# Two expert layers with sorted dispatch: each dispatch scatter waits for the landing of the one before it

## The chip, the core and the metric

The kernel runs on one core of a Trainium2 chip. The metric is the device time of one execution in microseconds, given as the median over runs. The core's engines are TensorE (PE, with its weight loads as PEld), VectorE (DVE), ScalarE (ACT), GpSimd (POOL) and SyncE (SP); "q" behind an engine's name is its own DMA queue or its instruction sequencer. DMAs issued by SyncE and by GpSimd are carried out by 16 shared DMA engines.

## What is computed

4096 tokens of width 128 (32 tiles of 128 tokens, in 128 batches of 32) pass two layers with a residual each. Cut to what matters:

```python
# layer 0: weights by batch, then 16 experts, one per token, and a shared expert
h   = einsum('bnc,bcd->bnd', x, w[subject]) + b[subject]
e   = top_1(h @ w_router.T);  s = sigmoid(logit of e)
y   = down_e(up * silu(gate)) of the row s*h  +  shared(h)
x   = x + y
# layer 1: adapter and norm by batch, then 8 experts, two per token, capacity 1280 rows each
h   = layernorm(x + relu(x @ W1[lang] + b1) @ W2[lang] + b2) * gamma + beta
y   = g1 * expert_e1(h) + g2 * expert_e2(h) + 0.1 * shared(h)   # a row past the capacity is dropped
x   = x + y
```

## The kernel before

**Dispatch.** Each layer sorts its tokens by expert in HBM. For each tile of 128 tokens VectorE computes a slot per token (`slot`), ScalarE copies the token rows, with a code and the score behind them, to `disp` (130 floats a row), and GpSimd issues one indirect DMA, a scatter, that writes the tile's 128 rows of 520 bytes to their slots in `rows0` (layer 0) or `rows1` (layer 1).

- Layer 0: 32 scatters at line 571, in four rounds of eight (`RT` = 8). A round begins when VectorE has its slots (`slots0`, line 918) and ScalarE its rows and scores. The scatters increment the semaphores `sc0[0]` and `sc0[1]`, by turns of four tiles (`G` = 4).
- Layer 1: 64 scatters at line 605, 32 for the tokens' first choice (`k` = 0) and 32 for the second. The first choice has rounds of 8, 8, 8, 4 and 4 tiles, each waiting for its slots (`slots1`, line 1072); the second choice's slots come all at once (line 1177). The semaphores are `sc1[k][half]`. Twice, GpSimd rewrites the codes of one half of `disp` between scatters (line 612).

Between the two dispatches GpSimd's program has the 48 scatters back of layer 0's results (line 582) and six residual additions (line 376); after them come the 80 scatters back of layer 1 (line 623).

**Who waits for a dispatch.** SyncE's program is in order too. It waits until all scatters of layer 0 have landed (both `sc0` at their full count), then loads blocks of 128 sorted rows (line 450, `blk_x`). In layer 1 it waits for all four `sc1` in the same way, then loads groups of 256 sorted rows (line 487, `grp_x`).

**TensorE.** In layer 0 it transposes x (line 1304), applies the weights by batch (line 1361), computes the router logits (line 1380), then the shared expert of six of the eight groups of four tiles (lines 1393 and 1402). Then come the 48 blocks: a transpose of the block as its first step (line 1304 with `blk_x`), gate and up (lines 1426 to 1428), down (line 1441). In layer 1 it runs adapter, norm and logits for eight groups (lines 1545 to 1589), the shared expert (up in lines 1517 to 1519, down in line 1603), of which most lies in a loop, and then 40 groups of sorted rows: a transpose (line 1304 with `grp_x`), up (lines 1633 to 1635), down (line 1645). Its first transpose of a group stands ahead of the last shared product.

VectorE's output of a group is `grp_y` (line 1236). At the end the results are read back, weighted and stored. SyncE also issues, early in layer 0, the zero fills of `rows0`, `rows1` and `back1` (lines 413, 426, 429) and the loads of all expert weights of layer 0 (lines 420 and 423).

Of the kernel before, what the change touches and what calls it, by code (L numbers as in the profile page):

```python
# [5 lines left out]
def adaln_moe_two_layers(  # L6
# [44 lines left out]
    S = T // B  # L51
    NSUB = c0_w.shape[0]
    E0, _, F0x2 = f0_gate_up.shape
    F0 = F0x2 // 2
    C0 = F0 // P
    NLANG = c1_b2.shape[0]
    A = c1_w1.shape[1] // NLANG
    E1, _, F1 = f1_w1.shape
    C1 = F1 // P
    TOP_K = 2  # L60
# [7 lines left out]
    NT = T // P  # L68
    G = 4
# [41 lines left out]
    with ctx:  # L111
# [3 lines left out]
        def sem(name):  # L115
            return ctx.enter_context(nc.semaphore(name))
# [174 lines left out]
        sc0 = [sem(f"sc0_{k}") for k in range(2)]  # L291
# [47 lines left out]
        sc1 = [[sem(f"sc1_{k}{h}") for h in range(2)] for k in range(2)]  # L339
# [190 lines left out]
        def _(pool):  # L530
# [35 lines left out]
            for t in range(NT):  # L566
                if t % RT == 0:
                    pool.wait_ge(slots0, t // RT + 1)
                    pool.wait_ge(scored, t // RT + 1)
                    pool.wait_ge(tok_done, (t + RT) // G)  # L570
                gp.indirect_dma_start(rows0, bass.IndirectOffsetOnAxis(ap=slot[:, 0, t:t + 1], axis=0),  # L571
                                      disp[:, t, :], None, bounds_check=NBLKP * P - 1,
                                      oob_is_err=False).then_inc(sc0[t // G % 2], 16)
# [22 lines left out]
            HT = NT // 2  # L596
            for k in range(TOP_K):
                for t in range(NT):
                    if k == 0 and t in first_tiles:
                        r = first_tiles.index(t)  # L600
                        pool.wait_ge(slots1, r + 1)
                        pool.wait_ge(b_tk, (t + round_tiles[r]) // G)
                    if k == 1 and t == 0:
                        pool.wait_ge(slots1, NR1 + 1)
                    gp.indirect_dma_start(rows1, bass.IndirectOffsetOnAxis(ap=slot[:, k, t:t + 1], axis=0),  # L605
                                          disp[:, t, :], None, bounds_check=E1 * CAP - 1,
                                          oob_is_err=False).then_inc(sc1[k][t // HT], 16)
                    if (k, t) in ((0, NT - 8), (1, HT - 8)):
                        h = k
                        pool.wait_ge(sc1[0][h], 16 * HT)  # L610
                        half = slice(h * HT, (h + 1) * HT)
                        gp.tensor_scalar(disp[:, half, H:H + 1], codes[:, half].unsqueeze(2), float(-T), None,
                                         ALU.add).then_inc(codes1, 1)
                        pool.wait_ge(codes1, h + 1)
# [687 lines left out]
        def _(pe):  # L1302
# [33 lines left out]
            for n in range(NG + 1):  # L1336
# [11 lines left out]
                if n < NG:  # L1348
                    pe.wait_ge(xT_done, n + 1)
                    if n == 0:  # L1350
                        pe.wait_ge(ld_c0w, 16)
                        pe.wait_ge(off_ready, 1)
                    _, offs = nc.values_load_multi_w_load_instructions(
                        w0off[0:1, n * GB:(n + 1) * GB], engines=(mybir.EngineType.PE,), min_val=0,
                        max_val=(NSUB - 1) * H, skip_runtime_bounds_check_because="subjects are under NSUB")
                    for b in range(QB):
                        if b == 1 and n >= 3 and n % 2 == 1:
                            rank0((n - 3) // 2)
                        for i in range(G):
                            t = i * QB + b  # L1360
                            last = mm(PS[1 + b][0:S, i * H:(i + 1) * H],  # L1361
                                      xT[n % 2][:, t * S:(t + 1) * S], c0w[:, ds(offs[t], H)],
                                      start=True, stop=True)
                        last.then_inc(pe_c, 1)
# [363 lines left out]
```

## Time and profile before

| | |
|---|---|
| Median of 3 runs | 573.94 us (572.52 to 575.43) |
| Span of the profiled execution | 571.1 us |
| TensorE, matmuls | 463.1 us, 81% of the span, 3132 instructions |
| VectorE | 261.9 us, 46% |
| ScalarE | 255.9 us, 45% |
| GpSimd | 238.0 us, 42%, 255 instructions |
| Granted TensorE clock, mean | 0.909 |
| DMA | 62.33 MB, 109 GB/s on the mean |

The profiled execution's own device time isn't given beside its span; the median of the runs lies 2.8 us above the span. Times in a trace count from the span's start. A row of the timeline has the start, the busy time, engine, line, operation, what it writes and reads, and in brackets how long the engine sat idle before and what ended that. "issue" is a time in which the engine waited for nothing that the profile shows. A transfer's own time isn't in its issuing row; the DMA views and the chain of waits show it. On 40 slices of the span a digit is a busy share in tenths.

### The profile page before, as it was taken

How to read it: one execution, taken by the hardware profiler on the slowest of the kernel's cores; microseconds unless marked ns; L12 is line 12 of the kernel's file. 1: busy time of each engine (PE TensorE's matmuls, PEld its weight loads, DVE VectorE, ACT ScalarE, POOL GpSimd, SP SyncE). 2: the span in 40 equal slices, each digit the busy share in tenths (PEclk: the TensorE clock that was granted, in tenths of full speed). 3: DMA queues.
4: the chain of work that ended last, by engine and by line, in shares of the span. 5: the costliest groups of instructions: out<-in, count | busy, mean ns of one | idle time of the engine just before them, and what ended most of it. 6: DMA issues, size and time to landing. Idle time of an engine off the chain costs nothing.

```text
span 571.1 us, 10130 instructions
## 1 busy us (share of the span) xinstructions
PE 463.1 (81%) x3132; PEld 392.7 (69%) x3133; DVE 261.9 (46%) x831; ACT 255.9 (45%) x596; POOL 238.0 (42%) x255
## 2 busy tenths in 40 slices
PE   6897698978888889999846765489999999999910
PEld 3785564566676766787744655178999999999900
DVE  1144267845555554347447912053433333233475
ACT  2453453235555543556314241034455555555653
POOL 2023535214554555003272777600155555556550
PEclk8997879999999999999787796579999999999975
DMA  9999921102222107400010111110223434313569
GB/s 242 365 340 368 367 66 37 39 23 67 74 71 63 47 11 235 143 2 20 19 51 15 48 48 55 42 47 1 61 76 96 134 107 113 105 50 88 165 182 282
DMA packets 70930, 62.33 MB, mean 109 GB/s; under 512 B 9676, under 2 KB 57439, under 8 KB 70898
## 3 DMA queue, kind: packets, MB, share of 16 engines
q1 hardware_dynamic: 63202, 48.32, 28.5%
q0 software_dynamic: 7168, 12.56, 6.7%
q10 hardware_dynamic: 528, 1.05, 0.6%
q8 instruction: 17, 0.28, 0.2%
q14 instruction: 15, 0.12, 0.1%
HBM read 32.44 MB, written 31.69 MB: 112 GB/s over the span
## 4 chain that ended last, share of the span: by engine, by line
PE 63%; another core or an unknown queue 10%; DVE 9%; DMA 7%; issue 6%; ACT 2%; POOL 1%; SPq 0%; DVEq 0%; POOLq 0%; ACTq 0%
PE PS L1645 11%; PE PS L1304 8%; PE PS L1361 6%; PE PS L1603 5%; PE PS L1441 3%; PE PS L1635 3%; PE PS L1565 3%; PE PS L1633 3%; PE PS L1634 3%; PE PS L1393 2%; PE PS L1402 2%; DMA back1b<-grp_y,grp_i 2%; PE PS L1426 2%; PE PS L1428 1%
## 5 line engine op out<-in xcount | busy, mean ns | idle before, releaser
L623 POOL DMA_INDIRECT back<-grp_y,grp_i x70 | 69.8, 997 | 93.9 <-DVE grp_y L1236 71.0
L605 POOL DMA_INDIRECT rows<-disp,slot x64 | 63.6, 994 | 76.1 <-DVE slot L1072 56.0
L1645 PE MATMUL PS<-w2r,act 128*128 128x128 f32 x640 | 78.1, 275 | 0.5 <-ACT act L789 0.5
L1645 PEld LDWEIGHTS PS<-w2r,act 128*128 128x128 f32 x640 | 74.8, 192 | 0.9 <-DVE grp_y L1236 0.7
L582 POOL DMA_INDIRECT back<-act,blk_i x48 | 46.9, 977 | 60.8 <-DVE act L1015 41.1
L789 ACT ACTIVATE act<-PS,b1r 128x256 f32<-128x256 f32 x160 | 63.7, 477 | 16.5 <-PE PS L1635 14.2
L571 POOL DMA_INDIRECT rows<-disp,slot x32 | 32.6, 1018 | 67.4 <-issue 53.8
L1236 DVE TENSOR_TENSOR grp_y<-PS,b2r 128x256 f32<-128x256 f32 x40 | 17.0, 424 | 89.6 <-PE PS L1645 69.5
L1603 PE MATMUL PS<-sw,act 128*128 128x128 f32 x256 | 37.5, 313 | 14.1 <-issue 11.8
L1633 PE MATMUL PS<-xh,w1h 128*128 128x256 f32 x160 | 48.3, 302 | 0.0
L740 ACT ACTIVATE act<-PS,sb 128x512 f32<-128x512 f32 x32 | 21.4, 688 | 59.6 <-remote 32.9
L1603 PEld LDWEIGHTS PS<-sw,act 128*128 128x128 f32 x256 | 36.5, 228 | 15.4 <-issue 13.5
L1635 PE MATMUL PS<-xh,w1l 128*128 128x256 f32 x160 | 45.2, 283 | 0.0
L643 ACT ACTIVATE xh<-PS 128x256 fp32r<-128x256 f32 (+1 forms) x48 | 20.1, 419 | 55.9 <-PE PS L1304 48.2
L1634 PE MATMUL PS<-xl,w1h 128*128 128x256 f32 x160 | 44.9, 281 | 0.0
L1361 PE MATMUL PS<-c0w,xT 128*32 x256 | 38.7, 321 | 7.4 <-issue 7.4
L1361 PEld LDWEIGHTS PS<-c0w,xT 128*32 128x32 f32 x256 | 32.5, 131 | 12.4 <-issue 9.3
L1441 PEld LDWEIGHTS PS<-w_dn,act 128*128 128x128 f32 x192 | 25.8, 190 | 15.5 <-issue 14.7
L1441 PE MATMUL PS<-w_dn,act 128*128 x192 | 30.9, 283 | 5.5 <-ACT act L643 5.2
L1008 DVE SCALAR_TENSOR_TENSOR act<-PS,blk_x,act 128x256 f32<-128x256 f32 x48 | 23.2, 483 | 20.2 <-ACT act L697 15.7
L643 ACT ACTIVATE t<-PS 32x512 f32<-32x512 f32 x32 | 18.7, 584 | 29.0 <-PE PS L1361 20.7
L1148 DVE SCALAR_TENSOR_TENSOR acc<-PS,acc 128x512 f32<-128x512 f32 x8 | 5.5, 690 | 54.9 <-remote 38.5
(256 smaller groups left out, 1009.9 us busy)
## 6 DMA issues: line engine op xcount, KB each, us to landing
rows<-zrow SPq DMA_DIRECT2D x32, 260.0 KB, 5.0
grp_x<-rows SPq DMA_DIRECT2D x40, 130.0 KB
w_raw<-in_f_gate_up SPq DMA_DIRECT2D x8, 512.0 KB, 10.1
back<-zrow SPq DMA_DIRECT2D x8, 512.0 KB
back<-back SPq DMA_DIRECT2D x16, 256.0 KB, 5.0
blk_x<-rows SPq DMA_DIRECT2D x48, 65.0 KB
acc<-in_x SPq DMA_DIRECT2D x8, 256.0 KB, 5.8
y0g<-back SPq DMA_DIRECT2D x8, 256.0 KB, 3.2
```

The source lines that it names most:

```text
L582: gp.indirect_dma_start(back0, bass.IndirectOffsetOnAxis(ap=blk_i[c][:, 0:1], axis=0), blk_y[s][:, :], None, bounds_check=last_token, oob_ ...
L605: gp.indirect_dma_start(rows1, bass.IndirectOffsetOnAxis(ap=slot[:, k, t:t + 1], axis=0), disp[:, t, :], None, bounds_check=E1 * CAP - 1, ...
L623: gp.indirect_dma_start(back, bass.IndirectOffsetOnAxis(ap=grp_i[v % NX][:, u:u + 1], axis=0), grp_y[k][:, u, :], None, bounds_check=last, ...
L789: sc.activation(act[k][:, c, 0:UP], PS[1 + k * (C1 // 2) + c // 2][:, (c % 2) * UP:(c % 2 + 1) * UP], ACT.Silu, bias=b1r[e][:, c:c + 1]).t ...
L1304: return nc.tensor.transpose(dst, src, ident[0:k, 0:k])
L1361: last = mm(PS[1 + b][0:S, i * H:(i + 1) * H], xT[n % 2][:, t * S:(t + 1) * S], c0w[:, ds(offs[t], H)], start=True, stop=True)
L1441: last = mm(PS[4 if k == 0 else 7][:, 0:H], blk_aT[k][:, c * P:(c + 1) * P], w_dn[:, ds(off + c * H, H)], start=c == 0, stop=c == C0 - 1)
L1603: last = mm(tile(PS[4], i), tile(act[k][:, c, :], i), sw2[:, c, :], start=c == 0, stop=c == C1 - 1)
L1633: mm(y, high, xh[k][:, 0:UP], start=True, stop=False)
L1634: mm(y, high, xl[k][:, 0:UP], start=False, stop=False)
L1635: last = mm(y, low, xh[k][:, 0:UP], start=False, stop=True)
L1645: last = mm(PS[5 + k][:, u * P:(u + 1) * P], act[k][:, c, u * P:(u + 1) * P], w2r[e][:, c, :], start=c == 0, stop=c == C1 - 1)
```

## The change

Ahead of each scatter but the first of a layer, GpSimd waits until the semaphore of the scatter before it has reached that scatter's count: 31 waits in layer 0, 63 in layer 1. The scatters, their order, their semaphores and all other engines' programs stay. In layer 1 the first scatter of the second choice waits for the last one of the first.

```diff
@@ layer 0 dispatch, GpSimd
                     pool.wait_ge(tok_done, (t + RT) // G)
+                if t >= 1:
+                    pool.wait_ge(sc0[(t - 1) // G % 2], 16 * ((t - 1) // (2 * G) * G + (t - 1) % G + 1))
                 gp.indirect_dma_start(rows0, bass.IndirectOffsetOnAxis(ap=slot[:, 0, t:t + 1], axis=0),
                                       disp[:, t, :], None, bounds_check=NBLKP * P - 1,
                                       oob_is_err=False).then_inc(sc0[t // G % 2], 16)
@@ layer 1 dispatch, GpSimd
                     if k == 1 and t == 0:
                         pool.wait_ge(slots1, NR1 + 1)
+                    if (k, t) > (0, 0):
+                        kl, tl = divmod(k * NT + t - 1, NT)
+                        pool.wait_ge(sc1[kl][tl // HT], 16 * (tl % HT + 1))
                     gp.indirect_dma_start(rows1, bass.IndirectOffsetOnAxis(ap=slot[:, k, t:t + 1], axis=0),
                                           disp[:, t, :], None, bounds_check=E1 * CAP - 1,
                                           oob_is_err=False).then_inc(sc1[k][t // HT], 16)
```

## Rows read from the trace of the kernel before

**Rows 1.** The page: its head, and the DMA business in 40 slices of 14.3 us

```profile
span 571.1 us, 10130 instructions
...
DMA  9999921102222107400010111110223434313569
```

**Rows 2.** The page, costliest groups: busy us, mean ns, idle before

```profile
L605 POOL DMA_INDIRECT rows<-disp,slot x64 | 63.6, 994 | 76.1 <-DVE slot L1072 56.0
```

**Rows 3.** Timeline of GpSimd, layer 0's dispatch: start us, busy us

```profile
38.86 1.18 POOL L571 DMA_INDIRECT rows<-disp,slot  x1 [33.99 <-issue]
...
79.30 0.98 POOL L571 DMA_INDIRECT rows<-disp,slot  x1 [11.31 <-issue]
80.58 0.98 POOL L571 DMA_INDIRECT rows<-disp,slot  x1 [0.30 <-issue]
...
93.86 0.98 POOL L571 DMA_INDIRECT rows<-disp,slot  x1 [4.59 <-DVE slot L918]
...
103.39 1.50 POOL L571 DMA_INDIRECT rows<-disp,slot  x1 [0.30 <-issue]
```

**Rows 4.** Timeline of GpSimd, layer 1's dispatch

```profile
265.26 0.99 POOL L605 DMA_INDIRECT rows<-disp,slot  x1 [36.61 <-DVE slot L1072]
...
284.99 0.97 POOL L605 DMA_INDIRECT rows<-disp,slot  x1 [9.79 <-DVE slot L1072]
...
309.64 1.37 POOL L605 DMA_INDIRECT rows<-disp,slot  x1 [9.64 <-DVE slot L1072]
...
368.15 0.98 POOL L605 DMA_INDIRECT rows<-disp,slot  x1 [0.30 <-issue]
```

**Rows 5.** Timeline of SyncE's queue: first block loads, first group loads

```profile
106.35 17.63 SPq L450 DMA_DIRECT2D blk_x<-rows  x6
...
370.50 31.80 SPq L487 DMA_DIRECT2D grp_x<-rows  x6
```

**Rows 6.** Timeline of TensorE: first block, two shared products, first group

```profile
119.56 0.33 PE L1304 MATMUL PS<-ident,blk_x 128*128 128x128 f32 x1 [0.78 <-DVE acc L964]
...
374.50 5.45 PE L1603 MATMUL PS<-sw,act 128*128 128x128 f32 x32 [0.82 <-DVE acc L1150]
...
382.60 3.73 PE L1603 MATMUL PS<-sw,act 128*128 128x128 f32 x32
...
398.92 0.38 PE L1304 MATMUL PS<-ident,grp_x 128*128 128x128 f32 x2
```

**Rows 7.** DMA queues, packets: 38.86 to 41.00; 38.86 to 43.00; 79.30 to 81.25

```profile
q1 hardware_dynamic: 300, 0.61, 104.1%
...
q0 software_dynamic: 37, 0.08, 6.7%
...
q0 software_dynamic: 32, 0.07, 10.4%
```

**Rows 8.** The chain of waits: start us, us of three transfers

```profile
122.83 1.82 DMA blk_x<-rows
...
211.68 2.08 DMA back<-act,blk_i
...
213.85 2.88 DMA y0g<-back
```

**Rows 9.** Timeline of VectorE: two steps that give slots to waiting GpSimd

```profile
92.89 0.17 DVE L918 CAST slot<-slotF 128x8 int32<-128x8 f32 x1
...
264.22 0.17 DVE L1072 TENSOR_SCALAR slot<-slotF 128x8 int32<-128x8 f32 x1
```

**Rows 10.** Three windows: length, busy us of PE, PEld, DVE, ACT, POOL; PEclk, DMA share, GB/s

```profile
336.90:344.60 7.70, 0.15 (x1) 0.00 (x0) 1.45 (x3) 0.07 (x1) 5.61 (x7) 0.73 0.13 43
350.00:372.60 22.60, 8.46 (x19) 4.70 (x19) 0.00 (x0) 1.38 (x2) 14.75 (x15) 0.58 0.17 54
374.50:398.90 24.40, 24.40 (x164) 22.77 (x165) 10.27 (x21) 9.12 (x14) 0.00 (x0) 0.93 0.00 1
```

## The prediction

> **What bounds the kernel now.** I began with the page: a span of 571.1 us, and the strip of DMA business, where the slices up to 71 us (five of 14.3 us each) stand at nine tenths and the rest far lower [rows 1]. The costliest groups show the edited instructions: the 64 scatters of L605, 63.6 us of work, 994 ns each [rows 2]. GpSimd is busy 42% of the span, so a share says little; what counts is whether the two dispatches end in time for whoever waits for all of them.
>
> I then followed GpSimd in order of time. In layer 0 it issues four rounds of eight scatters. The first scatter starts at 38.86. Within a round one follows the other at 1.28 us (0.98 of work, 0.30 of idle time), as from 79.30 to 80.58; between rounds it waits for slots; the last starts at 103.39 [rows 3]. In layer 1 the 64 scatters start at 265.26, the rounds whose slots come late at 284.99 and 309.64, and the last at 368.15 [rows 4]. SyncE waits for every landing of a layer and only then loads rows: it issues the first block load at 106.35 and the first group load at 370.50, which is 2.35 us after the start of the last scatter of layer 1 [rows 4, 5].
>
> Last I looked at the consumer. TensorE takes the first block at 119.56 and the first group at 398.92 [rows 6]. Neither waits for the dispatch. With a small load taking 1.82 us [rows 8], the first block has been there since about 108.3, so layer 0 has 11 us of slack. For layer 1 I take 2.4 us for the 130 KB group load, between 1.82 us for 65 KB and 2.88 us for 256 KB [rows 8]; it has been there since 372.9, so the slack is 26.0 us. The bound is now the chain of TensorE and the engines that feed it. The dispatch lies beside it, with these two slacks.
>
> **The change, part by part.** It removes nothing and moves nothing. It adds 31 waits in layer 0 and 63 in layer 1, all on GpSimd's queue, each for the landing of the scatter just issued. Semaphore and count name just that scatter, so no wait is satisfied early. Behind each wait stands the next scatter, so a chain of issue, landing and wake replaces a chain of issues. The cost of the 94 wait instructions themselves is taken as nothing: GpSimd would be waiting for the landing at that time anyway.
>
> *Landing, nothing else on the DMA queues.* The chain shows the last scatter back of layer 0 starting at 211.68 and landing 2.08 us later [rows 8]. It moves 512 bytes per row where the edited ones move 520. For the edited ones, all 32 packets of the scatter of 79.30 are done in the window that ends at 81.25, 1.95 us after its start [rows 7]; that is the lower bound, 1.9. SyncE's 2.35 holds its own reaction too [rows 4, 5]; that is the upper bound. I take 2.1.
>
> *Wake.* No row shows GpSimd woken by its own DMA. The nearest shows it woken by VectorE: the slots of L918 end at 93.06 and the scatter starts at 93.86, 0.80 us later [rows 3, 9]; L1072 ends at 264.39 and the scatter starts at 265.26, 0.87 us later [rows 4, 9]. The 0.30 between two scatters without a wait [rows 3] is the floor: there the next instruction is already at the engine, and with a wait it can't be. I take 0.8.
>
> So one cycle is **2.9 us** instead of 1.28, with bounds of 1.9 + 0.8 = 2.7 and 2.35 + 0.87 = 3.2.
>
> *Landing under load.* Until about 71 us other transfers fill the DMA engines [rows 1]. Of the first scatter, started at 38.86, no packet is seen by 41.00 and the 32nd only shortly before 43.00 (37 by then, some of them the second scatter's) [rows 7]. That is 4.1 us to land, and a cycle of 4.9. Five packets too many by then may mean a landing somewhat earlier, and the wait for the semaphore somewhat later: bounds 3.4 and 5.0 for the landing, 4.2 and 5.8 for the cycle. Seven cycles fall into this stretch: 38.86 + 7 × 4.9 = 73.2.
>
> The DMA page of the Trainium skill (DMA: Bandwidth & Descriptors, section Queues, rings and completion order) says that each DMA engine takes turns between its queues, packet by packet. By that rule a scatter with two packets on each engine would wait for two foreign ones, 0.12 us each (300 packets in 2.14 us on 16 engines) [rows 7], land after about 2.3 us and not 4.1, and the sum would be 12.6 us smaller, an estimate of 645 us. The trace disagrees with so small a delay.
>
> *Layer 0.* All later rounds have their slots (79.30, 93.86) before GpSimd gets to them. The last scatter starts at 38.86 + 7 × 4.9 + 24 × 2.9 = 142.8. Add 2.35 until SyncE issues and 1.9 for the load: TensorE takes the first block at 147.0 instead of 119.56, **+27.4 us**. The 11 us of slack are used up in this number.
>
> *Layer 1.* Every slot is ready before its turn again: round two would begin at 288.5 (ready at 284.99), the 25th scatter at 334.9 (ready at 309.64). Counted from the same start, the last one starts at 265.26 + 63 × 2.9 = 448.0. With 2.35 and 2.4 the first group is taken at 452.7 instead of 398.92, **+53.8 us**. The two copies of L612 between scatters ran while nothing waited for them; now they run during a landing, at no cost.
>
> *Clock.* TensorE now idles some 27 us before the blocks and much longer before the groups. After the idle stretch up to 374.50 one shared product took 5.45 us, and the next 3.73 us [rows 6]: 1.7 us for running below the full clock. Twice that is 3.4; the block stage is not bound by TensorE alone, so I take **3 us** in all.
>
> *The sum.* 27.4 + 53.8 + 3.0 = 84.2 us on a span of 571.1, so 655.3. The median of the runs, 573.94, is 2.8 above the span. That gives **658 us** for the changed kernel.
>
> *A gain that the longer cycle may bring.* While layer 1's scatters come every 1.28 us, TensorE is all but still from 336.9 to 344.6 and does little from 350 to 372.6; when they have ended it is busy all the time [rows 10]. If spaced scatters free it, it reaches the first group some 30 us earlier and waits there for the dispatch. I cost it at nothing, since the dispatch is then what comes last by 53.8 us or more.
>
> **The rivals.**
> A. *Short cycle.* GpSimd is woken by a landing almost as fast as it passes from one scatter to the next (0.30). The cycle is 2.4, under load 4.4. Layer 0: 38.86 + 30.8 + 57.6 + 4.25 = 131.5, +12.0. Layer 1: 265.26 + 151.2 + 4.75 = 421.2, +22.3. With the clock 37, so 611 us. For it: the 0.30 is a real row. Against it: both wakes on record are 0.80 or more.
> B. *The stillness of TensorE lasts as long as the scatters do*, or the cycle lies above 3.2. In the first case TensorE is only freed 4.5 us after the last scatter's start, as now (368.15 to 372.6), and still has the 26.3 us from there to 398.92 before it: 448.0 + 30.8 = 478.8, 26 us more than in the sum, 684 us. Against it: in the pauses between the rounds TensorE ran well, and the new cycle is pause for two thirds.
> C. *Load costs a scatter nearly nothing*: its few packets slip in between the others, the loaded cycle is 3.1 us and not 4.9, and 7 × 1.8 = 12.6 us go from the sum: 645 us. For it: a scatter has only two packets on each engine (32 in all) [rows 7]. Against it: the first scatter's late packets.
> D. *Faster.* The cycle is so short that the dispatch stays hidden, and TensorE's stillness goes. The point of decision: the last scatter of layer 1 must start by 398.92 − 4.75 = 394.2, so a cycle under (394.2 − 265.26) / 63 = 2.05 us. At 1.6 us, with the 25th scatter at 309.64, the last would start at 372.0 and the first group be taken at 376.8, 22 us earlier: 552 us. Against it: a landing alone was 2.08 us.
> E. *The waits pass early* and nothing changes: 574 us. Only a miscounted semaphore could do that.
>
> **How the numbers follow.** Forecast 0.60, A 0.13, B 0.16, C 0.07, D 0.03, E 0.01. At both lower bounds (2.7; 4.2) the sum is 38.86 + 29.4 + 64.8 + 4.25 = 137.3, +17.8, and 265.26 + 170.1 + 4.75 = 440.1, +41.2, with the clock 62: 636 us. At both upper bounds (3.2; 5.8) it is 160.5, +41.0, and 471.6, +72.7, with the clock 117: 691 us. The range takes these in and about half of A: 622 to 692 us. About 0.5% is what a measurement of this kernel can tell from no change. Faster by more than that is D, 0.03; within it E, 0.01; slower everything else, 0.96.
>
> **What the new profile would show.** Scatters of a round 2.7 to 3.2 us apart in both layers, wider apart before 71 us. SyncE's first block load near 145, and its first group load near 370.5 + 79.8 + 27.4 + 1.5 = 479. TensorE idle before the first block and before the first group, released there by the load. If scatters stand 2.4 us apart, A is right. If TensorE still does shared products after the first group has landed, B. If the first eight scatters are spaced like the rest, C. The prediction is wrong at its root if the first group is taken without a wait for the load.

## Result and profile after

| | before | after |
|---|---|---|
| Median, 4 runs each | 573.5 us | 687.65 us (685.92 to 689.23) |
| Ratio, 95% interval | | 1.2015 [1.1955, 1.2075] |
| Profiled execution, own time and span | -, 571.1 us | 686.79, 684.7 us |
| First block taken | 119.56 | 161.04 |
| First scatter of layer 1 | 265.26 | 307.74 |
| First group taken | 398.92 | 514.77 |
| From there to the end of the span | 172.2 | 169.9 |

The kernel is slower by 114 us. The forecast was 658, the range 622 to 692. Each ratio here and below is taken from executions in the chip's faster state alone and can differ by some tenths of a per cent from the quotient of the medians. The four differences between the lines of the table are +41.5, +1.0, +73.4 and -2.3; they sum to the 113.6 us between the spans.

The page, now in slices of 17.1 us, shows two holes in TensorE's strip: at 0 from 120 to 154 us and from 411 to 513. The DMA strip, nine tenths at the start as in [rows 1], is near nothing in both.

```profile
span 684.7 us, 10136 instructions
...
PE   6888893005888889999779910000009999999940
...
DMA  9999200001222207100000000000003343333198
```

The timeline of GpSimd after the change (start us, busy us, engine, line, operation, idle before and releaser), layer 0 and then layer 1, to be read against [rows 3, 4]:

```profile
41.46 1.18 POOL L573 DMA_INDIRECT rows<-disp,slot  x1 [36.53 <-issue]
48.25 0.98 POOL L573 DMA_INDIRECT rows<-disp,slot  x1 [5.61 <-DMA rows<-disp,slot]
...
72.70 0.97 POOL L573 DMA_INDIRECT rows<-disp,slot  x1 [2.77 <-DMA rows<-disp,slot]
75.76 0.97 POOL L573 DMA_INDIRECT rows<-disp,slot  x1 [2.09 <-DMA rows<-disp,slot]
...
91.87 0.97 POOL L573 DMA_INDIRECT rows<-disp,slot  x1 [2.32 <-DMA rows<-disp,slot]
96.95 0.98 POOL L573 DMA_INDIRECT rows<-disp,slot  x1 [4.10 <-DMA rows<-disp,slot]
...
156.77 0.97 POOL L573 DMA_INDIRECT rows<-disp,slot  x1 [2.18 <-DMA rows<-disp,slot]
...
307.74 0.99 POOL L610 DMA_INDIRECT rows<-disp,slot  x1 [36.61 <-DVE slot L1077]
310.84 0.98 POOL L610 DMA_INDIRECT rows<-disp,slot  x1 [2.11 <-DMA rows<-disp,slot]
...
510.08 0.98 POOL L610 DMA_INDIRECT rows<-disp,slot  x1 [2.07 <-DMA rows<-disp,slot]
```

Each scatter is now released by the landing of the one before. The first five cycles average (72.70 − 41.46) / 5 = 6.25 us (four of 6.6 to 7.2 and a fifth of 3.82), the next 26 average 3.23, and the 63 of layer 1 average (510.08 − 307.74) / 63 = 3.21 us.

The chain of waits splits one quiet cycle (start us, us, what):

```profile
141.24 2.29 DMA rows<-disp,slot
143.53 0.02 issue
143.55 0.03 POOLq L573
143.58 0.73 issue
144.31 2.29 DMA rows<-disp,slot
```

2.29 us from the scatter's start to its landing, 0.78 us until GpSimd starts the next: 3.07 us.

SyncE's queue and TensorE, against [rows 5, 6]:

```profile
159.19 19.28 SPq L450 DMA_DIRECT2D blk_x<-rows  x13
...
512.42 3.57 SPq L487 DMA_DIRECT2D grp_x<-rows  x6
```

```profile
161.04 0.45 PE L1309 MATMUL PS<-ident,blk_x 128*128 128x128 f32 x1 [50.87 <-DMA blk_x<-rows]
...
386.75 3.73 PE L1608 MATMUL PS<-sw,act 128*128 128x128 f32 x32
393.13 3.73 PE L1608 MATMUL PS<-sw,act 128*128 128x128 f32 x32
...
514.77 0.66 PE L1309 MATMUL PS<-ident,grp_x 128*128 128x128 f32 x2 [117.91 <-DMA grp_x<-rows]
```

TensorE waits 50.9 us for the first block and 117.9 us for the first group. That is more than the kernel lost. The shared products (line 1608) now follow each other every 6.38 us: the still stretches of [rows 10], in which TensorE was held up, are gone, and the time won there goes into the longer wait.

### The profile page after: what moved, and what is told of

Its sections match the earlier page's. It is cut to its first block, busy times and chain, and to the rows that moved or that the text cites. A ratio compares the mean times of both kernels' runs of the same rounds, so it can differ in the third digit from the quotient of the medians.

```text
span 684.7 us, 10136 instructions
## 1 busy us (share of the span) xinstructions
PE 450.3 (66%) x3132; PEld 385.8 (56%) x3133; DVE 260.0 (38%) x831; ACT 256.1 (37%) x596; POOL 235.7 (34%) x255
## 4 chain that ended last, share of the span: by engine, by line
DMA 40%; PE 38%; issue 14%; DVE 2%; ACT 2%; another core or an unknown queue 2%; POOLq 1%; SPq 0%; POOL 0%; DVEq 0%; ACTq 0%
DMA rows<-disp,slot 36%; PE PS L1650 8%; PE PS L1309 6%; PE PS L1446 3%; PE PS L1640 2%; PE PS L1639 2%; PE PS L1638 2%; PE PS L1366 2%; PE PS L1570 2%; PE PS L1431 2%; PE PS L1433 1%; DMA back1b<-grp_y,grp_i 1%; PE PS L1432 1%; DMA acc<-in_x 1%
## 5 line engine op out<-in xcount | busy, mean ns | idle before, releaser
L1309 PE MATMUL PS<-ident,grp_x 128*128 128x128 f32 x80 | 15.6, 278 | 119.2 <-DMA grp_x<-rows 117.9
L1309 PEld LDWEIGHTS PS<-ident,grp_x 128*128 128x128 f32 x80 | 10.0, 143 | 119.7 <-issue 119.2
L1309 PE MATMUL PS<-ident,blk_x 128*128 128x128 f32 x48 | 14.1, 293 | 56.3 <-DMA blk_x<-rows 51.1
L1216 DVE TENSOR_SCALAR grp_i<-grp_x 128x2 int32<-128x2 f32 x35 | 6.1, 174 | 115.3 <-DMA grp_x<-rows 115.3
L1309 PEld LDWEIGHTS PS<-ident,blk_x 128*128 128x128 f32 x48 | 7.0, 146 | 58.4 <-issue 57.5
L1366 PE MATMUL PS<-c0w,xT 128*32 x256 | 33.7, 294 | 8.1 <-issue 8.1
L1008 DVE TENSOR_TENSOR blk_xl<-PS,blk_xh 128x128 fp32r<-128x128 f32 x48 | 14.0, 291 | 65.6 <-ACT blk_xh L648 58.2
L648 ACT ACTIVATE blk_xh<-PS 128x128 fp32r<-128x128 f32 x48 | 13.2, 274 | 62.3 <-PE PS L1309 61.2
L1366 PEld LDWEIGHTS PS<-c0w,xT 128*32 128x32 f32 x256 | 29.5, 119 | 11.5 <-issue 10.0
```

Of the source, the lines that this page charges most:

```text
L648: return sc.activation(dst, src, ACT.Copy)
L1309: return nc.tensor.transpose(dst, src, ident[0:k, 0:k])
L1366: last = mm(PS[1 + b][0:S, i * H:(i + 1) * H], xT[n % 2][:, t * S:(t + 1) * S], c0w[:, ds(offs[t], H)], start=True, stop=True)
```

## Experiments

Ratios are to the kernel before as run beside each: medians 571.15 us for e1 to e4, 571.08 for e5 to e8, 574.25 for e9 to e11.

### Each layer's waits alone

e1 is the changed kernel without its wait in layer 1:

```diff
-                    if (k, t) > (0, 0):
-                        kl, tl = divmod(k * NT + t - 1, NT)
-                        pool.wait_ge(sc1[kl][tl // HT], 16 * (tl % HT + 1))
```

e2 is the changed kernel without its wait in layer 0:

```diff
-                if t >= 1:
-                    pool.wait_ge(sc0[(t - 1) // G % 2], 16 * ((t - 1) // (2 * G) * G + (t - 1) % G + 1))
```

> The 31 waits of layer 0 alone, layer 1 as before. Theory (a chain of issue, landing and wake that shows only past the slack): the first block is taken 41 to 42 us later than before, as in the changed kernel (161.0 against 119.6), and nothing else grows, since layer 1's scatters run at 1.28 us again: about 615 us. TensorE's still stretches in layer 1 are back. Rival (the two layers' costs are not additive: layer 0's delay is partly taken back by a shift of layer 1's work against its dispatch, or made larger by a cold clock): under 608 or over 622 us.

> The 63 waits of layer 1 alone, layer 0 as before. Theory: the dispatch takes 63 cycles of 3.2 us instead of 103 us in all, less the slack of 26 us: the first group is taken 73 us later than before relative to the dispatch's start, the work after it takes 2 us less, so about 645 us, and with e1 the two sum to the 114 us of the changed kernel. TensorE's shared products run through without a still stretch and then wait over 100 us for the first group. Rival (the still stretches come from what TensorE and ScalarE do and not from the scatters' spacing): TensorE still stands still for some 30 us, which costs no time here but is seen in the trace.

e1 took 612.33 us (ratio 1.0720 [1.0663, 1.0776]) and e2 644.89 us (1.1312 [1.1230, 1.1394]). That is 41.2 and 73.7 us over 571.15, together 114.9, against 114.15 for both. Both times are as expected, and the costs add: each is one dispatch past its own slack. In e1 the first block is taken at 161.07, and with scatters 1.28 us apart TensorE is held up again in layer 1: it sits idle for 13.56 us ahead of the shared product at 417.82. In e2 it is not held up, and then waits:

```profile
352.45 3.73 PE L1606 MATMUL PS<-sw,act 128*128 128x128 f32 x32
469.68 0.66 PE L1307 MATMUL PS<-ident,grp_x 128*128 128x128 f32 x2 [113.50 <-DMA grp_x<-rows]
```

### What makes the first landings late

The changed kernel, with the zero fills of lines 426 and 429 moved behind the first weight loads of layer 1.

```diff
-            for r in range(0, E1 * CAP, P * 4):
-                sp.dma_start(rows1[r:r + P * 4, :].rearrange("(p a) r -> p (a r)", p=P),
-                             zrow[:, 0:zw]).then_inc(zero1, 16)
-            for r in range(0, TOP_K * T, P * 8):
-                sp.dma_start(back1[r:r + P * 8, :].rearrange("(p a) h -> p (a h)", p=P),
-                             zrow[:, 0:8 * H]).then_inc(zero1, 16)
...
+            for r in range(0, E1 * CAP, P * 4):
+                sp.dma_start(rows1[r:r + P * 4, :].rearrange("(p a) r -> p (a r)", p=P),
+                             zrow[:, 0:zw]).then_inc(zero1, 16)
+            for r in range(0, TOP_K * T, P * 8):
+                sp.dma_start(back1[r:r + P * 8, :].rearrange("(p a) h -> p (a h)", p=P),
+                             zrow[:, 0:8 * H]).then_inc(zero1, 16)
             for k in range(TOP_K):
                 for h in range(2):
                     sp.wait_ge(sc1[k][h], 16 * (NT // 2))
```

> The changed kernel with the zero fills of rows1 and back1 (9.4 MB) issued behind layer 1's first weight loads instead of early in layer 0. Theory (the first scatters land late because the DMA engines are full of these fills): no cycle of layer 0 is 6 us any more, all are 3.1 to 3.4, the last scatter starts at about 141 instead of 156.8, and the kernel takes about 672 us. Rival (a landing of the first round is late for another reason, for instance the first use of the queue or ScalarE's and VectorE's work at that time): the first five cycles stay above 5 us and the time is 686 to 690 us. The fills at their new place may hold the start of layer 1's dispatch by a few us.

675.22 us, ratio 1.1823 [1.1758, 1.1889]: 11 to 12 us less than the change, by the ratios and by the medians (687.65, ratio 1.2015; measured at another time). GpSimd's timeline, layer 0:

```profile
39.46 1.18 POOL L573 DMA_INDIRECT rows<-disp,slot  x1 [34.58 <-issue]
45.47 0.98 POOL L573 DMA_INDIRECT rows<-disp,slot  x1 [4.83 <-DMA rows<-disp,slot]
49.70 0.98 POOL L573 DMA_INDIRECT rows<-disp,slot  x1 [3.25 <-DMA rows<-disp,slot]
53.25 0.97 POOL L573 DMA_INDIRECT rows<-disp,slot  x1 [2.57 <-DMA rows<-disp,slot]
```

The third cycle is 3.55, and the last scatter starts at 144.08. So the fills made most of the early landings late. The theory had wanted the first two cycles short too, and the first is still 6.0 us. Weight loads remain there: SyncE's queue fills 53% of the DMA engines' time in that cycle. That the first use of the queue is slow in itself, the rival's example, does not fit a later run: in e11, which also has the late fills, the first scatter starts 2.6 us later (42.07), and the third, which waits for it, starts at 45.56; less the 0.78 us of its wake, the first had landed within 2.7 us.

### A wait that reaches further back

Here each scatter waits for the one two before it. Two scatters are then in flight, so they need semaphores of their own: four by turns in each layer. These waits also cover the one ahead of line 612.

```diff
-        sc0 = [sem(f"sc0_{k}") for k in range(2)]
+        sc0 = [sem(f"sc0_{k}") for k in range(4)]
...
-            for k in range(2):
-                sp.wait_ge(sc0[k], 16 * (NT // 2))
+            for k in range(4):
+                sp.wait_ge(sc0[k], 16 * (NT // 4))
...
+                if t >= 2:
+                    pool.wait_ge(sc0[(t - 2) % 4], 16 * ((t - 2) // 4 + 1))
...
-                                      oob_is_err=False).then_inc(sc0[t // G % 2], 16)
+                                      oob_is_err=False).then_inc(sc0[t % 4], 16)
...
+                    f = k * NT + t - 2
+                    if f >= 0:
+                        pool.wait_ge(sc1[f // 2 % 2][f % 2], 16 * (f // 4 + 1))
...
-                                          oob_is_err=False).then_inc(sc1[k][t // HT], 16)
+                                          oob_is_err=False).then_inc(sc1[t // 2 % 2][t % 2], 16)
...
-                        pool.wait_ge(sc1[0][h], 16 * HT)
```

> In both layers each scatter waits for the landing of the one two before it, with four semaphores by turns. Theory: two landings overlap, so the cycle falls to half, 1.55 to 1.65 us outside the loaded stretch. Layer 0: round four starts with its slots at 94 and ends at 106 to 107, hidden as before. Layer 1: from the slots at 309 on 39 cycles of 1.6, the last scatter at about 372 against 368 before, first group landed at 377. If the wider spacing takes TensorE's still stretches away, it reaches the first group before that and the kernel gains up to 22 us: about 552 us. Rival (the spacing of 1.3 and 1.6 us is the same to TensorE; only pauses of 2 us free it): 573 to 577 us.

545.94 us, ratio 0.9567 [0.9502, 0.9632]: **faster than the kernel before.** Layer 1's scatters run from 257.55 to 366.12; those of the second choice stand 1.63 us apart on average, from 1.28 to 2.3; in layer 0 the first block is taken at 112.19. TensorE:

```profile
343.16 3.73 PE L1607 MATMUL PS<-sw,act 128*128 128x128 f32 x32
370.76 0.66 PE L1308 MATMUL PS<-ident,grp_x 128*128 128x128 f32 x2 [23.86 <-DMA grp_x<-rows]
```

It runs through at 6.38 us a shared product, is done at 346.9, and waits for the group. Measured from layer 1's first scatter the first group comes after 113.2 us, against 133.7 before. The dispatch has become a little longer (108.6 us from first scatter to last, 102.9 before), and the kernel shorter, because before the bound was what the dispatch did to the other engines. The rival is out. The theory's 552 us was 6 too many: it gave layer 0 no gain, and it kept the slots of layer 1 as late as before. The first block came 7.4 us earlier, and the 21st scatter of layer 1, which waits for slots, started 36.8 us after the first, against 44.4 before.

> As e3, but each scatter waits for the one three before it. A landing and wake take 3.07 us, three spacings of 1.28 take 3.84, so the wait is met nearly always and the spacing stays 1.28 us, except behind a late landing. If the spacing is what makes TensorE stand still, the still stretches are back and the time is 568 to 575 us. If it is a pile of scatters behind a late landing that does it, the limit of three is enough, the dispatch ends near 362, and the kernel takes 540 to 546 us.

The same with 3 for 2: 559.18 us, 0.9784 [0.9691, 0.9876], faster than before, though not surely by 2%. In the quiet part of layer 1 the spacing is 1.28 us, and the still stretches are back:

```profile
329.28 5.35 PE L1607 MATMUL PS<-sw,act 128*128 128x128 f32 x32 [3.74 <-issue]
...
361.20 6.41 PE L1607 MATMUL PS<-sw,act 128*128 128x128 f32 x32 [19.01 <-DVE acc L1154]
```

The first group comes 129.8 us after the first scatter of layer 1 (256.75, 386.58). The first block is at 111.96: layer 0, where landings under load spaced the scatters at some 2 us, kept its gain of 7.6 us, most of the 12. So of the two expectations the first is right for layer 1. Its time, 568 to 575 us, was missed, chiefly because layer 0 gained.

> The wait for the one two before, in layer 1 alone; layer 0 unthrottled. Theory: layer 1's gain of e3 stays (first group 113 us after the dispatch's start, against 134 before), and layer 0's 7 us of e3 go (first block at 119.6 against 112.2): 551 to 555 us. Rival (layer 0 gave nothing in e3, its block start was only earlier by chance): 544 to 548 us.

The wait in layer 1 alone: 551.97 us, 0.9695 [0.9619, 0.9771], first block at 118.41. e3 was 6.0 us better, and its first block came 6.2 us earlier; that is layer 0's share, though the two were measured at different times and their intervals overlap a little. Why layer 0 gains was not tested. It looks like the same effect: from 60 to 80 us VectorE is busy for 7.80 us in the kernel before and for 14.17 us in e3.

### Is it the wait or the spacing

Both start from the kernel before and change layer 1 alone. `idle` is a new buffer that nobody reads. e6:

```diff
                                           oob_is_err=False).then_inc(sc1[k][t // HT], 16)
+                    for i in range(3):
+                        c = 3 * (NT * k + t) + i
+                        gp.memset(idle[:, c:c + 1], 0.0)
```

> No added wait at all: behind each scatter of layer 1 GpSimd writes three single columns of an unused buffer, which should space the scatters at 1.6 to 1.8 us. Theory (TensorE's still stretches come from scatters without a pause, and any pause takes them away): layer 0 as before, the last scatter of layer 1 at about 376, no still stretch, first group at about 381, 555 to 558 us. Rival (only the wait for a landing frees the engines): the still stretches last as long as the scatters, TensorE is freed at about 380 with 26 us of its work to do, 578 to 584 us.

568.87 us, 0.9983 [0.9945, 1.0021]. My spacing failed: the three writes slipped into the 0.30 us between two scatters, which stood 1.31 us apart and not the 1.6 to 1.8 expected.

```profile
350.99 0.98 POOL L606 DMA_INDIRECT rows<-disp,slot  x1 [0.16 <-issue]
351.94 0.20 POOL L611 MEMSET idle<- 128x1 f32 x3
352.30 0.98 POOL L606 DMA_INDIRECT rows<-disp,slot  x1 [0.16 <-issue]
```

The still stretches stayed (15.07 us before the product at 369.39), and the time, expected at 555 to 558 us, did not change. It tells nothing of wait against spacing.

e9:

```diff
                                           oob_is_err=False).then_inc(sc1[k][t // HT], 16)
+                    for i in range(1):
+                        c = 1 * (NT * k + t) + i
+                        gp.memset(idle[:, c:c + 1], 0.0).then_inc(idled, 1)
+                        pool.wait_ge(idled, c + 1)
```

> e6 spaced the scatters at 1.31 us only and left spacing and wait untold apart. Here GpSimd writes one column behind each scatter of layer 1 and waits for that write, never for a landing, which should space them at 2.0 to 2.1 us. Theory (spacing is what counts): no still stretch, TensorE is through with the shared expert near 350 and waits; with the slots of the late rounds at about 300 the last scatter starts at 380 to 390 and the first group is taken at 385 to 395: 558 to 568 us. Rival (only a wait for a landing frees the engines): the still stretches stay while scatters are issued, TensorE resumes behind them with some 26 us of work: 585 to 595 us.

568.29 us, 0.9944 [0.9893, 0.9996], at the upper edge of the 558 to 568 expected. Here GpSimd waits only for its own small write, and most scatters stand 1.89 us apart:

```profile
342.54 0.98 POOL L607 DMA_INDIRECT rows<-disp,slot  x1 [0.80 <-POOL idle L612]
343.51 0.12 POOL L612 MEMSET idle<- 128x1 f32 x1
344.43 0.98 POOL L607 DMA_INDIRECT rows<-disp,slot  x1 [0.80 <-POOL idle L612]
```

```profile
348.81 3.73 PE L1609 MATMUL PS<-sw,act 128*128 128x128 f32 x32
393.59 0.66 PE L1310 MATMUL PS<-ident,grp_x 128*128 128x128 f32 x2 [41.04 <-DMA grp_x<-rows]
```

No still stretch, with no wait for any landing. TensorE is done at 352.5 and waits 41 us for a dispatch that takes 125.8 us from first scatter to last, 23 us more than before. So no wait for a landing is needed; a pause between scatters is enough. It also shows that the gain is a balance: at 1.28 TensorE is held up, at 1.89 the dispatch is late by nearly as much, and at a mean of 1.63 (e3) the kernel is faster than at either.

### Versions that beat both kernels

> e3 with e4's late fills. In e3 TensorE waited 4.3 us for the first block, since the loaded stretch spaced layer 0's first scatters at up to 5 us. Theory: with the fills gone from there the first block is ready before TensorE, 4 us less, unless the fills at their new place hold back layer 1's dispatch: 539 to 543 us. Rival (the fills then collide with layer 1's start and the loads of its first experts, and the dispatch, which is the bound there, starts later): 546 to 555 us.

e3 with the late fills of e4: 538.32 us, 0.9435 [0.9359, 0.9510], 0.7 us below the range expected. The first block is taken at 106.81 without waiting for its load, and the late fills did not hold up layer 1.

> e8 without the wait on the last 12 scatters of layer 1. In e8 TensorE is through with the shared expert at about the time of the 52nd scatter and then waits 24 us for the first group, so nothing is left there that a denser spacing could hold up. Theory: 12 cycles of 1.29 instead of 1.62 us, 4 us less than e8: 533 to 536 us. Rival (the still stretch is then TensorE's last shared product or delays SyncE and the group loads): no gain, 537 to 541 us.

The edit against e8:

```diff
-                    if f >= 0:
+                    if 0 <= f < 50:
```

> e8's kernel once more, beside e10 on the same chip, to compare the two: 536 to 540 us, as in e8.

e10 took 534.13 us, 0.9273 [0.9224, 0.9322], and e8's kernel, run again beside it as e11, 538.73 us, 0.9363 [0.9327, 0.9398]. The last 12 scatters are 1.29 us apart, while TensorE has nothing left to do:

```profile
336.48 3.73 PE L1607 MATMUL PS<-sw,act 128*128 128x128 f32 x32
360.84 0.66 PE L1308 MATMUL PS<-ident,grp_x 128*128 128x128 f32 x2 [20.63 <-DMA grp_x<-rows]
```

The expected 4 us came (4.6), and the two intervals do not overlap. e10 is 7% below the kernel before, and its bound in layer 1 is the dispatch.

## Why the prediction was right, and where it was off

**The mechanism and the place were right.** Waits turn the dispatch into a chain of issue, landing and wake; the first block and the first group are released by their loads; nothing on the way is hidden beyond the slack. Both slacks were as read: e1 and e2 cost what the longer dispatch is past them.

**Cycle, 2.9 us: measured 3.21 in the mean of layer 1, 3.07 in a quiet cycle.** This is the step that was mis-sized, and most of the miss. The mean lies just above the stated upper bound of 3.2, and so over the line that the prediction drew for the second case of rival B.
- The wake, taken as 0.8 from GpSimd's waits for VectorE, was 0.78. Rival A, a wake of 0.30, is out.
- The landing, taken as 2.1, was 2.29. I had called the 2.35 us to SyncE's first load an upper bound that holds SyncE's reaction. The chain now shows that reaction as 0.08 us, so nearly all of the 2.35 was the landing. The 2.08 of a scatter back, whose rows are 512 bytes and not 520, had drawn me down. The Trainium skill's fit for such DMAs (DMA: Bandwidth & Descriptors, section Anatomy of one DMA — SWDGE (gpsimd) path), 2.0 us and the bytes at 436 GB/s, gives an estimate of 2.15 us for 66.6 KB; this trace is 0.14 above it.
- On top come late landings, 0.14 us a cycle. The longest of them stand beside packets of an instruction queue. The cycle from 91.87 to 96.95 is 5.08 us, and in the window 94.00 to 94.50 the instruction queue moves one packet of 0.02 MB; the cycle from 359.89 to 364.52 is 4.63 us, with a like packet between 361.00 and 361.50:

```profile
q8 instruction: 1, 0.02, 10.9%
...
q8 instruction: 1, 0.02, 14.4%
```

The Trainium skill (Runtime: NRT & Kernel Launch, section Instruction fetch mechanics) calls instruction fetches mostly hidden. Whether these two were not is open: no run tests that the packet is the cause, and the traces speak on both sides. In e2 three cycles of layer 1 hold such a packet (those from 264.48, 293.00 and 316.34) and take 3.13, 3.22 and 3.10 us; after the change the cycle from 336.15, with one, takes 4.44, and the one from 307.74, also with one, 3.10.

In the sum: layer 1's 63 cycles took 202.3 us and not 182.7, +19.6.

**Landing under load, 4.1 us, seven cycles: measured 5.8 to 6.4 us, four cycles, and one of 3.03.** The chain of waits after the change:

```profile
41.46 5.99 DMA rows<-disp,slot
...
48.25 5.80 DMA rows<-disp,slot
...
54.84 6.44 DMA rows<-disp,slot
...
62.06 6.03 DMA rows<-disp,slot
...
68.88 3.03 DMA rows<-disp,slot
...
72.70 2.28 DMA rows<-disp,slot
```

No q0 packet of the first scatter (41.46) is seen by 43.90, 28 by 45.90, 32 only by 46.90. Before, four scatters had started by 43.00, where I stopped counting, so the 37 packets seen by then need not hold all of the first one's. The five cycles, 6.25 us on average, lie above the stated upper bound of 5.8, but there were only five: 31.2 us in all, close to the 34.3 for seven of 4.9. That the two errors met is luck. e4 shows that the load is the cause. Rival C is out, and with it the estimate of a landing after 2.3 us under load, 645 us in all.

**Layer 0 in all, +27.4: measured +41.5.** From first to last scatter 115.3 us and not 103.9; 26 quiet cycles of 3.23 where 24 of 2.9 stood. Another 2.6 us is a later start of the first scatter (41.46 for 38.86); e1, with the same waits, had it at 40.75. From the last scatter to the first block 4.27, foreseen 4.25; layer 1's counterpart 4.69, foreseen 4.75.

**Clock, +3: nothing to see.** The first shared product after the wait takes 4.91 us at a granted clock of 0.75 where the one at 386.75 takes 3.73 at 1.00, but the stretches outside the dispatches grew by +1.0 and -2.3. The term is inside what two executions differ by.

**The gain costed at nothing** was real and worth nothing here, for the reason given. The first case of rival B is out: TensorE's shared products run through in e3, e9 and after the change, with scatters 1.63, 1.89 and 3.21 us apart. The text weighed the stillness as a risk; it was an opening. With a shorter wait the same effect makes the kernel faster than before, which rival D had tied to a cycle under 2.05 us. e3, with 1.63 us and 545.94 us, is that rival, reached by another wait. The bound of 2.05 was for a dispatch still hidden; in fact the limit is where the late dispatch costs more than the still stretches did. In e9, at 1.89 us, the two about balance.

**A miscount of the rounds.** Layer 1's first choice has rounds of 8, 8, 4, 4, 4 and 4 tiles, not 8, 8, 8, 4 and 4, so the scatter at 309.64 [rows 4] is the 21st and not the 25th. The forecast does not change: with cycles of 2.9 the 21st would start at 323.3, still later than its slots. Rival D does: at 1.6 us its last scatter comes at 309.64 + 43 × 1.6 = 378.4, the first group at 383.2, and the kernel takes 558 us and not 552.

With the measured cycles in the prediction's own formula, 41.46 + 31.2 + 26 × 3.23 + 4.25 = 160.9 (+41.3), and 265.26 + 63 × 3.21 + 4.75 = 472.2 (+73.3), the sum is 573.9 + 114.6 = 688.5 us. These terms are read from the run that they are to explain, so this shows that the formula is complete, not that it predicts.

## What to carry to other kernels

When each DMA waits for the one before, price a cycle as start to landing plus wake, both from the stretch in which it will run, and multiply by the length of the chain; then take off the slack of whoever waits for the last. The release of an engine that waits for a landing measures it: the chain shows how little of that interval is its own reaction. And look at what a dense run of small DMAs does to the other engines before treating its length as the only thing that matters: the best pace here is neither the fastest nor one at a time.

## What the runs showed of the hardware

- GpSimd's scatters 1.28 or 1.31 us apart (before, e1, e5, e6) hold up TensorE, ScalarE and VectorE after some time: TensorE stood still for up to 19 us in one piece (e5), and VectorE did nothing from 350.00 to 372.60 in the kernel before. VectorE resumes 4.8, 4.6, 4.5 and 2.8 us after the start of the last scatter in these four. With scatters 1.63 us apart on average, 1.89 and 3.21 (e3, e9, after) it did not happen in layer 1's shared expert. Whether the spacing or GpSimd's own idle time between scatters (0.16 and 0.30 us in the first group, 0.80 in e9) decides, and by what way the engines are held up, stays open; no run tells.
- A scatter of 66.6 KB lands 2.29 us after its start on quiet DMA engines, and 5.8 to 6.4 us after it when SyncE's transfers fill them (four scatters after the change).
- GpSimd starts its scatter about 0.8 us after a release: 0.80 and 0.87 us after VectorE's slots, 0.80 after its own small write (e9), 0.78 after a landing. SyncE starts its load 0.08 us after a landing.
